# Order of the matmuls in a round of the last 8-wide attention: both score pairs after the first maxima

## The reference

```python
qkv = x @ w_qkv                       # x already layer-normed
q, k, v = jnp.split(qkv, 3, axis=2)   # each to B, 16 heads, T, 8
att = jnp.einsum('bhqd,bhkd->bhqk', q, k) * (1 / sqrt(8))
att = jnp.where(causal, att, -jnp.inf)
att = jax.nn.softmax(att, axis=-1)
out = jnp.einsum('bhqk,bhkd->bhqd', att, v)
```

## Time and profile before

| | us |
|---|---|
| three runs: median (lowest, highest) | 1894.47 (1889.12, 1911.62) |
| the profiled execution, its time | 1897.73 |
| its span in the trace | 1896.0 |

### The profile page before, as it was taken

How to read it: one execution, slowest core, us unless ns; L and a number is a source line. 1 busy time by engine, 2 the same in 40 slices (tenths; PEclk the granted TensorE clock), 3 DMA queues, 4 the chain that set the end, 5 groups by cost and what they waited for, 6 DMA issues and landing times. The chain is left out here.

```text
span 1896.0 us, 37330 instructions
## 1 busy us (share of the span) xinstructions
PE 1637.7 (86%) x12310; PEld 679.1 (36%) x12310; DVE 1312.5 (69%) x3162; ACT 1142.0 (60%) x1788; POOL 662.3 (35%) x1229
## 2 busy tenths in 40 slices
PE   5878788597899999999999888987699999999787
PEld 3321221243343333333333565544333333333233
DVE  6687888676677777777773246665598888889164
ACT  6699998543055555555556433333447777777755
POOL 6464655676222232322322001102412232232373
PEclk9799999799889999999999999898899999999997
DMA  8632334257322221313210410000612222222201
GB/s 239 135 68 55 64 65 126 56 126 169 69 45 52 57 64 41 79 43 67 53 42 24 144 45 1 0 0 22 204 28 44 49 49 49 50 49 65 49 26 45
DMA packets 91797, 125.90 MB, mean 66 GB/s; under 512 B 24501, under 2 KB 63797, under 8 KB 91398
## 3 DMA queue, kind: packets, MB, share of 16 engines
q1 hardware_dynamic: 89526, 121.17, 28.0%
q10 hardware_dynamic: 2096, 2.47, 0.5%
HBM read 75.90 MB, written 47.58 MB: 65 GB/s over the span
## 5 line engine op out<-in xcount | busy, mean ns | idle before, releaser
L1064 ACT ACTIVATE q_buf<-ps 128x1024 f32<-128x1024 f32 (+1 forms) x1152 | 864.1, 822 | 408.0 <-PE ps L939 401.2
L1129 POOL TENSOR_SCALAR_AFFINE_SELECT q_buf<-q_buf 128x256 f32<-128x256 f32 x768 | 364.7, 499 | 731.6 <-ACT q_buf L1064 601.0
L1186 DVE TENSOR_REDUCE o_sb<-ps 128x2 f32<-128x1024 f32 (+1 forms) x544 | 503.6, 969 | 103.0 <-PE ps L963 70.4
L997 PE MATMUL ps<-q_buf,v_buf 128*9 128x512 f32 (+7 forms) x4608 | 462.1, 496 | 58.7 <-POOL q_buf L1129 53.9
L939 PE MATMUL ps<-q_buf,k_buf 49*128 49x512 f32 (+3 forms) x1536 | 311.7, 506 | 0.0
L939 PE MATMUL ps<-q_buf 48*128 48x512 bf16 (+7 forms) x1536 | 260.1, 331 | 33.9 <-ACT q_buf L1064 27.0
L1174 DVE CUSTOM_DVE_ANT_0 pr_buf<-ps,causal_row 128x384 f32<-128x384 f32 (+3 forms) x512 | 223.4, 488 | 85.1 <-PE ps L963 82.4
L1246 DVE TENSOR_SCALAR q_buf<-q_buf 128x1024 f32<-128x1024 f32 x288 | 218.0, 765 | 57.4 <-ACT q_buf L1064 53.0
L997 PEld LDWEIGHTS ps<-q_buf,v_buf 128*9 128x9 f32 (+1 forms) x4608 | 94.0, 95 | 247.5 <-issue 135.0
L939 PEld LDWEIGHTS ps<-q_buf,k_buf 49*128 49x128 f32 x1536 | 133.8, 187 | 129.6 <-issue 54.5
L939 PEld LDWEIGHTS ps<-q_buf 48*128 48x128 bf16 (+1 forms) x1536 | 75.4, 94 | 282.2 <-ACT q_buf L1064 225.0
(11 more groups left out here) (187 smaller groups left out, 1648.8 us busy)
## 6 DMA issues: line engine op xcount, KB each, us to landing
q_buf<-qm_d SPq DMA_DIRECT2D x32, 384.0 KB, 6.9
qm_d<-pr_buf SPq DMA_DIRECT2D x80, 128.0 KB, 2.4
o_d<-pr_buf SPq DMA_DIRECT2D x16, 512.0 KB, 2.7
q_buf<-o_d SPq DMA_DIRECT2D x8, 1024.0 KB, 5.1
q_d<-q_buf SPq DMA_DIRECT2D x48, 128.0 KB, 2.1
k_d<-q_buf SPq DMA_DIRECT2D x48, 128.0 KB, 1.9
k_buf<-km_d SPq DMA_DIRECT2D x32, 192.0 KB, 6.7
q_buf<-q_d SPq DMA_DIRECT2D x60, 96.0 KB
```

The costliest lines, as they stand in the source:

```text
L997: mm = nc.tensor.matmul(ps[VW * j:VW * j + V_ROWS_OUT, o_bank + half % O_BUFS, lo * P:(lo + nq) * P], v, units(i, r, j)[:, 0, off * P:(off ...
L1064: nc.scalar.activation(units(i, g, WIDE * e, WIDE), ps[:, bank:bank + WIDE, :], ACT.Exp, scale=scale).then_inc(s_e, 1)
L1129: nc.gpsimd.affine_select(out=blk, in_=blk, compare_op=ALU.is_ge, fill=0.0, base=0, pattern=[[0, 2], [1, P]], channel_multiplier=-1)\
L1186: nc.vector.tensor_reduce(to, sc, AX_X, ALU.max).then_inc(s_mr, 1)
```

## The change

In a1 the first pair of maxima is written ahead of the four scores of the round, instead of between the second and the third; the second pair stays behind the fourth score and ahead of the value row. A round was: two scores, first maxima, two scores, second maxima, value row. It is now: first maxima, four scores, second maxima, value row. The latent attention keeps its order, and rounds without maxima are the same. No instruction is added or removed.

```diff
                         for g in range(ROWS_P):
                             ahead = max_row(g, last) if has_max else None
+                            if ahead is not None and not latent:
+                                max_pair(n, b, i, *ahead, 0)
                             for e in range(EXPS_R):
                                 score_unit(n, i, g, e)
                                 done = WIDE * (e + 1)
-                                if ahead is not None and done % 2 == 0:
+                                if ahead is not None and (latent and done % 2 == 0 or not latent and done == QUAD):
                                     max_pair(n, b, i, *ahead, done // 2 - 1)
```

## The result

| | before | after |
|---|---|---|
| median of the runs | 1891.8 us | 1951.74 us |
| lowest, highest | 1888.93, 1911.62 | 1950.18, 1959.66 |
| span of the profile | 1896.0 us | 1948.5 us |

The ratio is 1.0296 (95% interval 1.025 to 1.0341): slower; the quotient of the two medians, 1.032, lies inside that interval. Run again on another occasion, the changed kernel had 1950.97 us and a ratio of 1.0263 (1.0217 to 1.0308). The forecast was 1946 us, a ratio of 1.027 to the median it was made against.

A forecast was written before the change was run, and what follows sets the result against it. It took TensorE, with one 1.17 us latency per round, to bound a1; fourteen items 49.4, plus 2.1 for item 14, less 1.3 hidden, gave +50 us: 1946 us, range 1926 to 1971.

The forecast's parts named there:

- The latency of 1.17 us: In each a1 round, first to fourth score is a fixed 1.17 us; TensorE work inside is free, outside is paid.
- The price of the pair: First pair ahead of score 1 adds 0.22, 0.50 or 0.55 us (no, four, eight masks), 3.53 us an item.
- VectorE's slack: At the gathering of an item's maxima, VectorE has about 0.5 us to spare, so it adds nothing.
- TensorE's wait for ScalarE: Idle ahead of the fourth score, about 0.56 us in nearly every round, growing from 18.7 to some 65 to 75 us.
- VectorE's idle time: Sign of being right: VectorE's idle time ahead of the reductions in a1 grows by about 50 us.
- Item 0: In its rounds 0 to 2 VectorE is behind from the warm-up, so 1.3 us of added time are hidden.
- The clock: Nothing added for a1; rival, chance 0.05: it falls, 13 us at 0.97, 111 us if half the time at lower level.
- a granted clock below 1.0: Sign of being wrong: in a1 the profile after the change shows the clock below its full level.
- VectorE's pace: Rival, chance 0.09: VectorE's reductions set a1's pace and hide the first pair's place, so time stays at 1898 us.
- score 4 does not come sooner: Denies the rival, chance 0.03, that scores together bring a1's fourth score sooner, saving some 42 us, to 1856.

The follow-up runs named there:

- 1: Kernel before, with the first maxima pair moved from behind the second score to behind the third: 1899.34 us, ratio 1.0022 to the kernel before.
- 2: Kernel before, with the causal masks left out of each row's first maxima pair: ratio 1.0015 to the kernel before.
- 3: Changed kernel, with the causal masks left out of each row's first maxima pair: median 1938.7 us, ratio 1.0209 to the kernel before.
- 5: The changed kernel run again, nothing else altered: 1950.97 us, ratio 1.0263 to the kernel before.
- 9: Kernel before, with four PSUM banks for scores instead of three and three for maxima, used singly, instead of four: ratio 1.0457.
- 10: Changed kernel, with four PSUM banks for scores instead of three and three for maxima instead of four: ratio 1.0255 to the kernel before.
- 4: Kernel before, reordered: two scores, first pair, third score, value row, fourth score, second pair: ratio 0.9981 to the kernel before.
- 6: As 4, with ScalarE's output copy moved from behind a round's first exponential to behind the previous round's fourth: 1880.69 us, ratio 0.9903 to the kernel before.
- 7: Order first pair, three scores, value row, fourth score, second pair, with the earlier output copy of 6: ratio 1.0016 to the kernel before.
- 8: Order two scores, first pair, third score, second pair, fourth score, value row: 1884.62 us, ratio 0.9938 to the kernel before.

## Why the prediction was right, and where it was off

The mechanism held point by point.

- **The latency of 1.17 us** did not move: 1.16 or 1.17 at the full clock in every round behind the first value row, of every kind, after the change and in numbers 1, 2, 3 and 5 (in the few at half level up to 1.41). That it is a bank wait is shown by numbers 9 and 10, where the fourth score follows the first by 0.45 to 0.90 and 0.22 to 0.49 us in the rounds with maxima; that what lies inside is free, by 1 and 2; that it is paid outside, by 3.
- **The price of the pair**: 0.22, 0.50, 0.55 us were taken, 0.22, 0.50, 0.56 measured. 3.53 us an item were forecast, 3.55 to 3.56 measured at full clock (28.63 and 28.64 in the two profiles of the changed kernel, less 25.08).
- **VectorE's slack** at the gathering was enough: no wait of TensorE for it in the repeating rounds.
- **TensorE's wait for ScalarE** was to be 65 to 75 us and is 67.7.
- **VectorE's idle time** was to grow by about 50 us and grew by 40: its waits for maxima are 81.2 us from 1405 to 1795 us, where 1405 to 1750 us had 41.3 before (the second line there, not in the earlier trace rows, is 13.2). Its busy time grew by the rest, from 314.96 us to 324.50: two reductions back to back took 2.37 us, and one by itself takes 1.23 (at 1633.82 us after the change).
- **Item 0** was mis-sized. The 1.3 us of its first three rounds were to be hidden, VectorE being behind anyway. From the last warm-up pair to the first value row it was 1394.62 to 1402.31, 7.7 us, and is 9.8, 2.1 more; first before, then after:

```profile
1394.62 0.39 PE L963 MATMUL ps<-q_buf 48*128 48x512 bf16 x2
...
1399.36 0.69 PE L939 MATMUL ps<-q_buf 51*128 51x256 bf16 x4
1400.27 0.40 PE L963 MATMUL ps<-q_buf 48*128 48x256 bf16 x4 [0.22 <-DVE o_sb L1186]
```

```profile
1393.70 0.39 PE L963 MATMUL ps<-q_buf 48*128 48x512 bf16 x2
...
1400.01 0.55 PE L963 MATMUL ps<-q_buf 48*128 48x256 bf16 x4 [0.71 <-DVE o_sb L1188]
...
1403.53 1.04 PE L997 MATMUL ps<-q_buf,v_buf 128*9 128x512 f32 x4
```

TensorE waits for VectorE ahead of the third round's first pair, and only then may issue the scores behind it; in the old order the first two stood ahead of that wait. What stays behind score 1 (the latency) is then added to VectorE's lateness instead of running beside it. Part of the 2.1 us is the clock, which in this execution was at half level from 1400.1 instead of 1401.3 us. No run separates it, but rows at full level give an estimate. The same round of a later item takes 2.49 us from its first pair to its value row (1634.63 to 1637.12), and here it takes 3.52: 1.0 us is the clock. In the kernel before, the second pair takes 0.64 us to the value row at full level (1628.48 to 1629.12) and 0.91 here: 0.3. That leaves 0.7 of the 2.1 to the clock and 1.4 to the order, about the 1.3 that these rounds cost anywhere else. So nothing was hidden.

- **The clock.** Nothing was added for it, with a chance of 0.05 for it as a rival. A form milder than the one priced there came true (3.4 us by the sum below, against 13), and a granted clock below 1.0 was named as a sign of being wrong. Two stretches at half level lie in the repeated items after the change, none before; one of them, in the view of stages:

```profile
1615.20:1618.60 3.40, 3.40 (x19) 0.59 (x19) 2.46 (x3) 1.76 (x4) 0.91 (x4) 0.50 0.04 6
```

Here 0.50 is the granted clock. The item around it is 30.25 us long, 1.6 more than its neighbours; the other likewise, and in the second profile of the kernel there is one such full item and two stretches in the last rounds. The Trainium skill ("TensorE: Matmul & The Clock Gate", the section on PSUM queue cycling) says that frequent short idles between groups can make the clock swing. The traces agree in kind, not in degree: the mean over the stage is 0.99, and idle time was there in every round while most rounds ran at full clock. Counted over the thirteen items behind item 0, the stretches at half level are two, one and two in the three profiles with the changed order and three score banks (after, 5 and 3), and none in the kernel before and in numbers 1, 2, 4, 6, 7 and 8. Number 9 has eleven, a mean clock of 0.95 from 1448 to 1841 us, and ten of its last twelve items at 30.2 us and longer, against 28.85. Number 10, which also waits in every round, has one. That the idle time brings the stretches on fits this count; no run shows it by itself.

From the first value row of the stage (1402.31, after the change 1403.53) to the one that starts at 1792.49 (1847.66) the profiles have 390.2 and 444.1 us, 53.9 more: fourteen times 3.55 is 49.7, the last two rounds with maxima behind that 0.8, the clock 3.4. With 2.1 for item 0 that is 56; the whole span grew by 52.5, because in this execution the last warm-up pair came 0.9 us sooner and the time behind the stage's last rounds was 2.7 us shorter. The medians show +56 and +60. The forecast of +50 is short of the first by the clock and item 0; the 4 us between the two occasions are not explained.

The rivals on the other side fell. VectorE's pace hides nothing, and score 4 does not come sooner with the scores together.

## What to carry to other kernels

In an engine's stream written by hand, look for the wait that repeats in every round and ask whether its length is a latency (it stays when the work inside it changes) or a sum of work. Work inside a latency is free and becomes fully paid as soon as it is moved out, so the price of this reordering could be read from the trace before: the moved piece's own time, times the rounds. The cure goes the same way: put more work into the gap (number 6, 1% faster than before), but check each buffer that the moved work needs sooner. Number 4 kept 0.26 us an item, since a copy came one exponential late; with the copy moved it was 0.79, since VectorE's banks came next; 1.3 had been forecast.

## What was not expected of the hardware

A short stretch at half clock costs nearly all that it can, although TensorE idles in every round. At half speed an engine that never waits would lose 1.7 us in a stretch of 3.4; the items around such stretches are 1.6 us longer. In number 9 the thirteen items behind item 0 are 17.8 us longer than at 28.85 each, which is 1.6 for each of their eleven stretches.

And the distance from first to fourth score is the same to 0.01 us at full clock in the orders of before, after and numbers 1, 2, 3 and 5, whether there is no other work between the scores or a maxima pair of 0.55 us. It gives way only to work that does not fit: with both pairs inside (number 8) it is 1.16 to 1.28 us without masks and 1.44 to 1.70 with them.
